# A graph kernel's fourth edge stage: 128-row contractions replaced by pairs of 64-row contractions

## What is computed

```
h = relu(layernorm(x))
q = h @ Wq                                    # per node, 8 heads of 16
k[e] = wk[e] * sum_s sh[e,s] * (h[src[e]] @ Cqk[:, s, :])      # s = 0..8
v[e] = wv[e] * sum_s sh[e,s] * (h[src[e]] @ Cv[:, s, :])
attn = segment_softmax(q[dst] . k)            # per head, over the edges of a node
out  = h @ W_self + segment_sum(v * attn) @ W_out, then a batch norm
```

## Time and profile before

| | |
|---|---|
| three runs | 3128.04, 3128.79, 3133.41 us; median 3128.79 |
| the profiled execution, from its first to its last instruction | 3126.1 us |
| the fourth edge stage in it | from the first fetch of source rows at 1878 us to the last addition at 3062 us |
| in it, between 2000 and 3000 us | PE 99.3% busy, DVE 87.4%, POOL 71.1%, transfers 88% of the 16 DMA engines, granted TensorE clock 1.00 |

### The profile page before, as it was taken

How to read it: one execution, slowest core, us unless ns; L and a number is a source line. 1 busy time by engine, 2 the same in 40 slices (tenths; PEclk the granted TensorE clock), 3 DMA queues, 4 the chain that set the end, 5 groups by cost and what they waited for, 6 DMA issues and landing times. The chain is left out here.

```text
span 3126.1 us, 51454 instructions
## 1 busy us (share of the span) xinstructions
PE 2476.7 (79%) x14006; PEld 2130.6 (68%) x14006; DVE 2209.2 (71%) x5060; ACT 864.2 (28%) x2414; POOL 2032.3 (65%) x2119
## 2 busy tenths in 40 slices
PE   5778787525667667477777767999999999999986
PEld 4777787424666666355555556888888888888862
DVE  4555555526888887555555563888888888888875
ACT  1111111136666663111111110222232222323231
POOL 4777777457777771277777736777776677677710
PEclk9776667657888888599999978999999999999985
DMA  3443333133333330155555557889888898888820
GB/s 84 94 89 86 86 87 86 30 68 64 61 60 60 60 52 4 46 155 160 152 160 152 160 147 179 214 206 214 212 206 205 203 216 206 207 204 205 213 68 11
DMA packets 333760, 404.38 MB, mean 129 GB/s; under 512 B 171136, under 2 KB 203006, under 8 KB 333570
## 3 DMA queue, kind: packets, MB, share of 16 engines
q1 hardware_dynamic: 252034, 251.20, 34.4%
q0 software_dynamic: 66560, 96.41, 14.5%
q10 hardware_dynamic: 14976, 54.53, 5.1%
HBM read 339.81 MB, written 62.07 MB: 129 GB/s over the span
## 5 line engine op out<-in xcount | busy, mean ns | idle before, releaser
L1934 PE MATMUL psum<-ckv,z 128*128 128x256 f32 x4160 | 967.8, 383 | 0.0
L1934 PEld LDWEIGHTS psum<-ckv,z 128*128 128x128 f32 x4160 | 766.7, 191 | 97.9
L1768 POOL DMA_INDIRECT acc<-QW,dst_i x416 | 399.5, 960 | 184.6 <-issue 111.2
L234 POOL DMA_INDIRECT ga<-TA,src_i x416 | 412.4, 991 | 161.6 <-issue 126.5
L1789 POOL DMA_INDIRECT ga<-XX,src_i x416 | 399.5, 960 | 162.8 <-issue 122.5
L1027 POOL DMA_INDIRECT ga<-T,src_i x416 | 401.9, 966 | 151.5 <-issue 125.9
L234 POOL DMA_INDIRECT ga<-T,src_i x416 | 396.6, 953 | 149.3 <-issue 124.7
L2048 DVE TENSOR_TENSOR z<-psum,shb 128x2560 f32<-128x2560 f32 x104 | 293.2, 2820 | 66.7 <-PE psum L1925 66.5
L1121 PE MATMUL psum<-HT,wy 128*128 128x128 f32 x1664 | 264.7, 324 | 70.0 <-DVE wy L1394 69.2
L445 PE MATMUL psum<-wre,re 128*128 128x68 f32 x832 | 215.2, 351 | 119.4 <-DVE oneT L290 67.7
L1121 PEld LDWEIGHTS psum<-HT,wy 128*128 128x128 f32 x1664 | 242.8, 232 | 87.8 <-DVE wy L1394 81.5
(11 more groups left out here) (362 smaller groups left out, 4142.9 us busy)
## 6 DMA issues: line engine op xcount, KB each, us to landing
shb<-in_ea SPq DMA_DIRECT2D x104, 640.0 KB, 6.2
WKV<-wkvo ACTq DMA_DIRECT2D x104, 512.0 KB
shb<-in_ea SPq DMA_DIRECT2D x104, 512.0 KB, 8.5
wkv<-WKV SPq DMA_DIRECT2D x104, 512.0 KB
dl<-DL SPq DMA_DIRECT2D x208, 128.0 KB
win<-TB SPq DMA_DIRECT2D x416, 32.0 KB
ga<-T,src_i POOLq DMA_INDIRECT x832
ef<-in_ea SPq DMA_DIRECT2D x104, 128.0 KB
```

What stands on the lines that cost most here:

```text
L234: pool.indirect_dma_start(o, None, table, bass.IndirectOffsetOnAxis(ap=src_i[:, g * GT + t:g * GT + t + 1], axis=0)).then_inc(s_g[k], 16)
L1768: pool.indirect_dma_start(qg[:, (g % QR) * GT + t, :], None, QW, bass.IndirectOffsetOnAxis(ap=dst_i[:, g * GT + t:g * GT + t + 1], axis=0) ...
L1934: last = pe.matmul(kv_of(k)[:, t, :], z[:, k % 2, j, t * 128:(t + 1) * 128], ckv[:, j, :], start=(j == 0), stop=(j == NZ - 1))
```

## The change

The contraction runs over nine steps of 64 rows, one per harmonic, on two tiles at once: tiles 0 and 1 of a group lie on partitions 0 to 63, tiles 2 and 3 on partitions 64 to 127. `z` and `shb` hold nine slices of 256 columns in place of five of 512. For each pair (a and 2+a) the loop alternates between the upper and the lower half of the array; the two write to different PSUM banks. A group has 72 passes, with 64 rows each. One transpose now serves two tiles, since a row of XX holds the features once and two tiles lie side by side in `ga` (`slot_of` gives the order). The products of a step come in two blocks of 36 passes in place of four of 10, so half 1 of the sums stands at the end of the step in place of three quarters into it. The harmonics come in another layout from the host: one row of 9 x 256 values per half group. `h` is written once into the space of `shb`, ACT's copy is gone, and the first harmonics loads stand behind XX's landing and the node transposes.

```diff
-        NZ = 5
+        NZ = 9
+        HW = GT * W // 2
-        XX = dram("XX", [N, 2 * D])
+        XX = dram("XX", [N, D])
-        ga = tmp("ga3", [128, GR * GT, F])
+        ga = tmp("ga3", [128, GR * GT, D])
-        shb = tmp("shb", [128, 2, NZ, GT * W])
-        z = tmp("z", [128, 2, NZ, GT * W])
+        shb = tmp("shb", [128, 2, NZ, HW])
+        z = tmp("z", [128, 2, NZ, HW])
-        twice = nodes[:, NJ * D:3 * NJ * D].rearrange("p (j a f) -> p j a f", j=NJ, a=2)
+        slot_of = lambda t: t % 2 * 2 + t // 2
+        hn = shb[0:PN].rearrange("p a z e -> p (a z e)")[:, 0:NJ * D].rearrange("p (j f) -> p j f", j=NJ)
...
                 def harmonics_load(i, k):
                     wait(sp, e3_z, g - 1)
-                    sp.dma_start(shb[0:D, k % 2], A["ea9"][0:NS:2, cols].partition_broadcast(D)).then_inc(e3_e[k % 2], 16)
-                    sp.dma_start(shb[D:128, k % 2, 0:NZ - 1], A["ea9"][1:NS:2, cols].partition_broadcast(D)).then_inc(e3_e[k % 2], 16)
+                    for half in range(2):
+                        sp.dma_start(shb[half * D:half * D + D, k % 2].rearrange("p z e -> p (z e)"),
+                                     A["ea9"][g * 2 + half:g * 2 + half + 1, :].partition_broadcast(D)).then_inc(e3_e[k % 2], 16)
...
-                for k in range(2):
-                    harmonics_load(0, k)
                 for k in range(2):
                     weights_load(0, k)
                 for h, (J, _) in enumerate(HALVES):
-                    sp.wait_ge(n3_x, h + 1)
+                    sp.wait_ge(n3_h, h + 1)
...
+                sp.wait_ge(n3_ox, len(HALVES) * 16)
+                sp.wait_ge(n3_t, len(R3))
+                for k in range(2):
+                    harmonics_load(0, k)
                 for part in PARTS:
...
-                for h, (J, _) in enumerate(HALVES):
-                    act.wait_ge(n3_h, h + 1)
-                    act.activation(twice[:, J, 1, :], twice[:, J, 0, :], ACT.Copy).then_inc(n3_x, 1)
...
-                    for t in range(GT):
-                        last = pe.transpose(bank[0][:, t * 128:(t + 1) * 128], ga[:, (k % GR) * GT + t, :], ident[:])
+                    for a in range(2):
+                        slot = (k % GR) * GT + 2 * a
+                        last = pe.transpose(bank[0][:, a * 128:(a + 1) * 128], ga[:, slot:slot + 2, :].rearrange("p a f -> p (a f)"), ident[:])
...
                     for j in range(NZ):
-                        last = pe.matmul(kv_of(k)[:, t, :], z[:, k % 2, j, t * 128:(t + 1) * 128], ckv[:, j, :],
-                                         start=(j == 0), stop=(j == NZ - 1))
+                        for half in range(2):
+                            rows = slice(half * D, half * D + D)
+                            last = pe.matmul(kv_of(k)[:, 2 * half + a, :], z[rows, k % 2, j, a * 128:(a + 1) * 128], ckv[rows, j, :],
+                                             start=(j == 0), stop=(j == NZ - 1))
...
-                    dve.tensor_tensor(z[:, k % 2], bank[0][:].unsqueeze(1).to_broadcast([128, NZ, GT * W]), shb[:, k % 2],
+                    dve.tensor_tensor(z[:, k % 2], bank[0][:, 0:HW].unsqueeze(1).to_broadcast([128, NZ, HW]), shb[:, k % 2],
                                       ALU.mult).then_inc(e3_z, 1)
```

More of the change, by code:

```diff
@@ L1694, in build @@
         sel_b = sb("sel_b", [24, 128])
-        XX = dram("XX", [N, 2 * D])
+        XX = dram("XX", [N, D])
         QW = dram("QW", [N, F])
-        n3_l, n3_p, n3_dve, n3_var, n3_std, n3_t, n3_tc, n3_q, n3_qc, n3_ox, n3_oq, n3_h, n3_x = [sem("n3_" + x) for x in
-            ("l", "p", "dve", "var", "std", "t", "tc", "q", "qc", "ox", "oq", "h", "x")]
+        n3_l, n3_p, n3_dve, n3_var, n3_std, n3_t, n3_tc, n3_q, n3_qc, n3_ox, n3_oq, n3_h = [sem("n3_" + x) for x in
+            ("l", "p", "dve", "var", "std", "t", "tc", "q", "qc", "ox", "oq", "h")]
         NL3 = 9
@@ L1712, in build @@
         e3_n = [sem(f"e3_n{k}") for k in range(2)]
-        (e3_one, e3_oa, e3_X, e3_z, e3_wq, e3_V, e3_ev, e3_s, e3_S, e3_acc, e3_M, e3_Mx, e3_i, e3_pad) = [
+        (e3_one, e3_oa, e3_X, e3_z, e3_wq, e3_V, e3_ev, e3_s, e3_S, e3_acc, e3_M, e3_Mx, e3_i) = [
             sem("e3_" + x) for x in
-            ("one", "oa", "X", "z", "wq", "V", "ev", "s", "S", "acc", "M", "Mx", "i", "pad")]
+            ("one", "oa", "X", "z", "wq", "V", "ev", "s", "S", "acc", "M", "Mx", "i")]
         S3 = softmax_sems("b3", bank[7])
@@ L1825, in _ @@
                 for m, w in ((ckv[:, :, 0:F], "Cqk"), (ckv[:, :, F:2 * F], "Cv")):
-                    L(m[0:D, :, :], A["L3_gnn_" + w][:, 0:NS:2, :])
-                    L(m[D:128, 0:NZ - 1, :], A["L3_gnn_" + w][:, 1:NS:2, :])
-                for k in range(2):
-                    harmonics_load(0, k)
+                    for half in range(2):
+                        L(m[half * D:half * D + D, :, :], A["L3_gnn_" + w])
                 for k in range(2):
@@ L1923, in transposes, with products @@
                     wait(pe, e3_z, g)
-                    for t in range(GT):
-                        last = pe.transpose(bank[0][:, t * 128:(t + 1) * 128], ga[:, (k % GR) * GT + t, :], ident[:])
+                    for a in range(2):
+                        slot = (k % GR) * GT + 2 * a
+                        last = pe.transpose(bank[0][:, a * 128:(a + 1) * 128], ga[:, slot:slot + 2, :].rearrange("p a f -> p (a f)"), ident[:])
                     last.then_inc(e3_X, 1)
-                def products(i, k, t):
+                def products(i, k, a):
                     g = i * UG + k
-                    if t == 0:
+                    if a == 0:
                         pe.wait_ge(e3_z, g + 1)
@@ L1933, in products @@
                     for j in range(NZ):
-                        last = pe.matmul(kv_of(k)[:, t, :], z[:, k % 2, j, t * 128:(t + 1) * 128], ckv[:, j, :],
-                                         start=(j == 0), stop=(j == NZ - 1))
-                    if t == GT - 1:
-                        last.then_inc(e3_V, 1)
+                        for half in range(2):
+                            rows = slice(half * D, half * D + D)
+                            last = pe.matmul(kv_of(k)[:, 2 * half + a, :], z[rows, k % 2, j, a * 128:(a + 1) * 128], ckv[rows, j, :],
+                                             start=(j == 0), stop=(j == NZ - 1))
+                            if a == 1 and j == NZ - 1:
+                                last.then_inc(e3_V, 1)
                 def body(i, k):
@@ L1948, in body @@
                         softmax_pe_0(pe, S3, q, 8, am3[:, b])
[L1949 to L1964, removed]
+                    if kv:
+                        products(*kv, 0)
+                    if old:
+                        sums(*old, 0)
+                    if p1:
+                        softmax_pe_1(pe, S3, q, 8)
+                    if p2:
+                        softmax_pe_3(pe, S3, q, 8)
+                    if kv:
+                        products(*kv, 1)
+                    if old:
+                        sums(*old, 1)
+                    if p1:
+                        softmax_pe_2(pe, S3, q, 8)
+                    if p2:
+                        pe.wait_ge(S3["less"], q + 1)
+                        softmax_pe_4(pe, S3, q, fac_cols, 8, sel8, 2)
                 def node_transposes(r):
@@ L1970, in node_transposes @@
                     for j in range(n):
-                        last = pe.transpose(bank[r % 2][0:D, j * PN:(j + 1) * PN], twice[:, j0 + j, 0, :], ident[0:PN, 0:PN])
+                        last = pe.transpose(bank[r % 2][0:D, j * PN:(j + 1) * PN], hn[:, j0 + j, :], ident[0:PN, 0:PN])
                     last.then_inc(n3_t, 1)
@@ L1997, in _ @@
                 pe.wait_ge(n3_qc, len(R3))
-                pe.wait_ge(n3_p, 4)
+                pe.wait_ge(n3_p, 3)
                 pe.sem_inc(e3_S, SPARE)
@@ L2030, in _ @@
                 for J, _ in HALVES:
-                    dve.scalar_tensor_tensor(twice[:, J, 0, :], XC[:, J, :], 0.0, st[:, 5, J].unsqueeze(2).to_broadcast([PN, J.stop - J.start, D]),
+                    dve.scalar_tensor_tensor(hn[:, J, :], XC[:, J, :], 0.0, st[:, 5, J].unsqueeze(2).to_broadcast([PN, J.stop - J.start, D]),
                                              ALU.max, ALU.mult).then_inc(n3_h, 1)
@@ L2046, in harmonics @@
                     dve.wait_ge(e3_e[k % 2], i * (UG // 2 * 32) + (k // 2 + 1) * 32)
-                    wait(dve, e3_V, g - 1)
-                    dve.tensor_tensor(z[:, k % 2], bank[0][:].unsqueeze(1).to_broadcast([128, NZ, GT * W]), shb[:, k % 2],
+                    wait(dve, e3_V, (g - 1) * 2)
+                    dve.tensor_tensor(z[:, k % 2], bank[0][:, 0:HW].unsqueeze(1).to_broadcast([128, NZ, HW]), shb[:, k % 2],
                                       ALU.mult).then_inc(e3_z, 1)
@@ L2251 @@
     a["ea64"] = np.pad(a.pop("edge_attr_64"), ((0, fill), (0, 0))).T
-    a["ea9"] = np.pad(a.pop("edge_attr_9"), ((0, fill), (0, 0))).T
```

(2 more changed lines are left out.)

10 lines of the change are left out of this document (3 added, 7 removed).

## The result

| | before | after |
|---|---|---|
| median of the runs | 3131.10 us (4 runs) | 3171.34 us (4 runs) |
| profiled execution, span | 3126.1 us | 3169.6 us |
| mean z to z, from the eleventh z to the last | 10.83 us | 11.11 us |

The ratio is 1.0126, with a 95% interval of 1.0112 to 1.0140: slower by 40 us, where the forecast was slower by 13. It lies inside the range and outside the likeliest case's own range of 3115 to 3165.

What follows compares the result with a forecast made beforehand. PE was taken as the bound (busy 993 of 1000 us). (0.80 - 0.60) / 4 = 0.05 us a step, 5 us over about 100 steps, 13 with the start: 3139 span, 3142 us median; range 3075 to 3290.

Steps and rivals of the forecast that it cites:

- the likeliest case: The forecast itself: kernel slower by 13 us, 3142 us, own range 3115 to 3165, chance 0.46.
- The step that failed: Half 1 of the sums at step's end: DVE's plain step 8.46 against PE's 10.60, so PE waits for nothing.
- Products, the stream: PE's 72 passes a step: 0.11 a pass, 4.18 a block, 8.36 a step, 0.39 less than 8.75.
- Changes of mode: PE between 64-row products and all-row transposes or sums: four changes a step at 0.20 us each, 0.80.
- the faster rival: Cheaper mode changes on PE: hidden drains give 3069, half price about 3100; gains below 0.17 a change; chance 0.24.
- Late `M3`: PE's first sums in one plain step: their wait for DVE's M3 goes, 0.6 us less a cycle.
- DVE's multiplication: Multiplication by harmonics: 2304 elements for 2560, 2.82 to 2.54 us, 0.28 less, no gain while PE bounds.
- Start: Harmonics loads ahead of QW in SP's queue: QW lands at 1902, 8 us late, bounds 0 and 10.
- Loads in strict order: Rival: no weight load passes a waiting matmul, 0.165 a pass, 4.0 us a step, 3540 us; chance 0.12.
- half overlap: Rival: weight loads of the two array halves hinder each other, 0.125 a pass, some 3250 us; chance 0.12.
- no overlap: Rival: the two array halves never work at once, 7.5 us a step more, 3890 us; chance 0.06.
- The clock: Sign for the fourth stage: if the granted clock's row falls below 1.00, none of the forecast holds.

Runs made afterwards that it cites:

- the extra ones: Changed kernel with each block of products cut in two and the sums' halves behind the first and third quarter, six mode changes a step, not four: 3141.07 us.
- the kernel with 41.40: Changed kernel with the second half of the sums right behind the first, ahead of the second block of products: 3097.11 us, ratio 0.9889.

## Why the prediction came out as it did

The sign and the range were right, and the way there was not: one step failed, one term was mis-sized the other way, and they partly cancel. That the kernel became slower as forecast is luck: it is slower by a wait that the forecast put at nothing, and without that wait it is faster than before (3123.84 and 3097.11 us).

- **The step that failed** is "DVE has that room ... and the transposes and products of the next step wait for nothing in that stretch", with "The softmax matmuls stay". DVE has the room, but the next step's PE row isn't transposes and products alone: in every fourth step L675 stands between them, and it needs two copies that DVE runs behind its additions. The forecast held DVE's sum of busy time against PE's and didn't follow what the first instruction of DVE's next step releases; its own sign, additions of half 1 that wait for sums at the end of a step, did come up, and was called harmless. Measured: 2.1 us a cycle, 47.5 us in all by moving the copies alone.
- **Products, the stream**, was too dear. Put at 4.18 a block, it takes 18 pairs at 0.215, 3.87; the forecast let the second half run one pass behind the first and added that pass at the end. In the trace the two halves start 0.01 us apart (2486.142 and 2486.149). Two pass starts every 0.215, as both limits of 0.11 said.
- **Changes of mode**: 0.17 each as the extra ones show it, 0.20 put down. The four of a step, added up from the rows of after, are what is left of 10.01 without the sums (twice 0.61), two transposes (0.22) and 36 pairs (7.74): 0.83, the 0.80 that was forecast. So the plain step failed low by the stream alone, 10.01 for 10.60; by the prediction's own mark (below 10.4, the price of the change has failed) one would have blamed the wrong term. The rule of the Trainium skill in TensorEngine Tiling (Array Packing), section Tiling Modes, that a change of mode drains the engine, agrees with these rows: 0.35 us for there and back.
- **The point from which the faster rival decides**, 0.17, was of no use: with 0.17 to 0.21 a change the loop did get faster once the wait was gone. The rival with cheaper changes had PE's step about right (9.80 to 10.20, measured 10.01), but by the wrong term: the changes cost what was forecast, and the stream was cheaper.
- **Late `M3`**: gone, as forecast; 0.60 in the kernel before with both halves of its sums in the middle, and no such wait in the stretch of after.
- **DVE's multiplication**: 2.55 for 2.54. By its busy time (832 of 1000 us) DVE was no bound; PE waited for the order of its work.
- **Start**: 8 forecast, 12.2 at the first query row, 12 to 15 by undoing it. The order of the transfers was right. What was left out is that four more harmonics loads come in while QW is under way; POOL gets QW's rows at 1908.6, not 1902.

```profile
1895.00:1900.00 5.00, 5.00 (x44) 4.34 (x42) 2.56 (x1) 0.00 (x0) 0.00 (x0) 0.88 1.02 285
```

  At that time the transfers run at 285 GB/s and at a share of 1.02, beyond the 215 of the earlier trace rows, so it was not a slow rate. By an estimate the amount accounts for it: eight loads of 576 KB and QW's 1562 KB in the 26.8 us from 1881.81 on are 236 GB/s, with 208 to 285 in the windows between 1885 and 1905. No run takes away the four later loads alone, so their part is not shown by itself.
- **Loads in strict order, half overlap, no overlap**: not so in the alternating order, where pairs start every 0.215. The second half's first load starts 0.01 us behind the first half's, ahead of the first half's second pass: six loads of 0.18 us or more each lie within 0.52 us.

```profile
2486.14 0.52 PEld L1936 LDWEIGHTS psum<-ckv,z 64*128 64x128 f32 x6 [0.17 <-issue]
```

- **The clock**: by the prediction's own sign, a row below 1.00, "none of this holds". The row is 0.99. The four falls follow the wait ahead of L675 and are gone with it, so they belong to the failed step and not to the stream.

Summed up on the loop: where the sums stand alike, a cycle fell from 42.71 to 41.40. From there to the 44.44 of after are 3.04 us. The waits ahead of L675 and L694 are 2.4 of them (2.5, less some 0.15 of waiting that the kernel with 41.40 has too), the falls of the clock nearly 0.3, and some 0.4 stay open. Together they gave back more than the change and the late `M3` had gained, so 43.31 became 44.44.

## What to carry to other kernels

When an instruction moves later on one engine, follow it through the engine that waits for it to the first thing that this engine releases next, in each kind of step of the cycle, also the rare ones; a share of busy time says nothing of that order. Here the gain on the bounding engine was given back by one wait of 2 us in every fourth step, and moving two copies ahead in DVE's order took the wait away. Put work that forces a change of tiling mode in one place of the step (0.35 us for two more changes here), and keep the passes of two tiles alternating in the program.

## What was not expected of the hardware

- Weight loads of the two halves run beside each other. In the earlier trace rows a load follows another after 0.11 us; here the loads of the two halves start 0.01 us apart, six lie within 0.52, and PE's pairs start every 0.215. The limit of 0.11 a load, which the half-overlap rival leaned on, is not shared between the halves.
- A wait of 2.1 us on PE, once in a cycle of 44 us, was followed by a fall of the granted clock to 0.50 in four of 23 cycles, and the products behind it took 5.5 us in place of 4.2. With the wait gone the stretch had no such fall.
- Passes of 64 rows one after the other, on one half and then on the other, were granted 0.50 of the clock for the whole stage, with PE busy throughout; the same passes in pairs were granted 0.99. What of it decides was not tried further.
- With all passes of one half first in the program and those of the other behind them, the second half started with three passes of the first still to start, and no earlier: matmuls of two halves do not start strictly in program order, but here they ran only three passes ahead.
